# Xattn and FFN block on one core: the router with its gate stationary in four column groups, and another order behind the last attention unit

## What is computed

```python
x = x + attention(layernorm(x), ctx, ...)          # [8, 128, 512]
xf = layernorm(x).reshape(-1, 512)
routing = softmax(xf @ gate_w.T, axis=1)           # 8 experts
in_scale, out_scale = routing @ in_channel_scale, routing @ out_channel_scale
out = (xf * in_scale) @ sign(weight).T * out_scale + bias
x = x + out
```

## Time and profile before

| | |
|---|---|
| median of 3 runs | 800.29 us |
| the profiled execution, its own time | 800.21 us |
| its span in the trace | 798.4 us |
| TensorE matmuls busy | 793.6 us, 99% |
| TensorE weight loads | 675.5 us, 85% |
| VectorE | 633.1 us, 79% |
| ScalarE | 352.9 us, 44% |
| GpSimd | 298.5 us, 37% |
| granted TensorE clock | 1.00 |

### The profile page before, as it was taken

How to read it: one execution, slowest core, us unless ns; L and a number is a source line. 1 busy time by engine, 2 the same in 40 slices (tenths; PEclk the granted TensorE clock), 3 DMA queues, 4 the chain that set the end, 5 groups by cost and what they waited for, 6 DMA issues and landing times.

```text
span 798.4 us, 12698 instructions
## 1 busy us (share of the span) xinstructions
PE 793.6 (99%) x4090; PEld 675.5 (85%) x4090; DVE 633.1 (79%) x1066; ACT 352.9 (44%) x949; POOL 298.5 (37%) x279
## 2 busy tenths in 40 slices
PE   9999999999999999999999999999999999999998
PEld 7888888888888888888888888888888888888886
DVE  6877878886893596889988879788877978877775
ACT  6633432432341253554534345343534434446683
POOL 3123021020111032746455446554544654434136
PEclk9999999999999999999999999999999999999999
DMA  8464674575456648627566666656665675653002
GB/s 302 146 200 171 223 247 137 177 256 171 154 183 212 210 160 274 212 68 233 168 216 206 195 183 200 224 153 212 199 213 154 207 225 159 200 195 139 1 1 106
DMA packets 103217, 145.54 MB, mean 182 GB/s; under 512 B 9944, under 2 KB 74584, under 8 KB 97648
## 3 DMA queue, kind: packets, MB, share of 16 engines
q1 hardware_dynamic: 102720, 144.33, 55.7%
q10 hardware_dynamic: 432, 0.39, 0.2%
HBM read 93.31 MB, written 51.38 MB: 181 GB/s over the span
## 4 chain that ended last, share of the span: by engine, by line
PE 98%; DMA 1%; DVE 0%; issue 0%; ACT 0%; SPq 0%; DVEq 0%
PE out L1470 11%; PE out L1472 11%; PE out L1471 11%; PE proj L1470 11%; PE proj L1472 11%; PE proj L1471 10%; PE s L1564 7%; PE o L1591 4%; PE s L1471 4%; PE s L1472 4%; PE s L1470 4%; PE t L1591 3%; PE proj L1667 1%; PE proj L1668 1%; PE t L1619 1%; PE t L1575 1%
## 5 line engine op out<-in xcount | busy, mean ns | idle before, releaser
L872 POOL TENSOR_TENSOR w_stage<-w_stage 128x256 f32<-128x256 f32 x30 | 26.9, 898 | 262.9 <-DMA w_stage<-in_wk 241.4
L896 POOL TENSOR_TENSOR bias_mask<-bias_raw,mask_neg 128x512 f32<-128x512 f32 x64 | 75.3, 1184 | 81.4 <-DVE s L1306 67.4
L1042 ACT ACTIVATE s<-s,neg_max 128x128 f32<-128x128 f32 x208 | 71.5, 349 | 52.5 <-DVE neg_max L1309 52.5
L1470 PE MATMUL out<-wo_hi,o_hi 128*128 128x512 f32 x224 | 88.5, 395 | 0.0
L1472 PE MATMUL out<-wo_lo,o_hi 128*128 128x512 f32 x224 | 87.8, 392 | 0.0
L1471 PE MATMUL out<-wo_hi,o_lo 128*128 128x512 f32 x224 | 87.3, 390 | 0.0
L1470 PE MATMUL proj<-x_hi,w_hi 128*128 128x512 f32 x210 | 85.0, 405 | 0.0
L884 POOL TENSOR_TENSOR w_lo<-w_stage,w_hi 128x512 fp32r<-128x512 f32 (+1 forms) x52 | 59.4, 1155 | 68.1 <-ACT w_hi L988 68.1
L1472 PE MATMUL proj<-x_lo,w_hi 128*128 128x512 f32 x210 | 82.5, 393 | 0.0
L1471 PE MATMUL proj<-x_hi,w_lo 128*128 128x512 f32 x210 | 82.0, 390 | 0.0
L1347 DVE TENSOR_TENSOR acc<-out,acc 128x512 f32<-128x512 f32 x100 | 67.2, 673 | 14.1 <-PE out L1472 14.0
(11 more groups left out here) (370 smaller groups left out, 2123.5 us busy)
## 6 DMA issues: line engine op xcount, KB each, us to landing
k_spill<-ring SPq DMA_DIRECT2D x64, 256.0 KB, 3.4
v_spill<-ring SPq DMA_DIRECT2D x64, 256.0 KB, 2.5
p_turned<-probs SPq DMA_DIRECT2D x208, 64.0 KB, 2.8
probs_t<-p_turned SPq DMA_DIRECT2D x52, 256.0 KB, 2.9
big_stage<-in_wv SPq DMA_DIRECT2D x8, 1024.0 KB, 8.7
w_stage<-in_wq SPq DMA_DIRECT2D x32, 256.0 KB, 3.5
k_first<-k_spill SPq DMA_DIRECT2D x8, 1024.0 KB, 7.3
v_first<-v_spill SPq DMA_DIRECT2D x8, 1024.0 KB, 9.7
```

The lines of the kernel that those rows point to most:

```text
L896: pool.tensor_tensor(bias_mask[:, j % 2], bias_raw[:, i % 2][:, None, :].to_broadcast([P, HALF, P]), mask_neg[:, halves[half], :], ALU.add ...
L1042: last = act.activation(scores_of(j)[:, b], scores_of(j)[:, b], ACT.Exp, bias=neg_max[:, col:col + 1], accum_out=row_sum[:, col:col + 1])
L1470: pe.matmul(to[:], left_hi, right_hi, start=first and n == 0, stop=False, skip_group_check=True)
```

## The change

The router's logits come about in another way. The gate becomes the stationary operand, padded with zeros to 32 columns (`COLS`), and the tile's transposed chunk is the moving one, 128 columns. A pair has two tiles of four chunks, so eight matmuls; they go to four groups of 32 columns of the array, and so to four groups of 32 partitions of `t_bank`, two chunks summed in each (G). VectorE copies that bank's 128 columns to SBUF (GC), and one matmul with a constant matrix of zeros and ones adds the chunks and turns the result to token by expert (GF); its 16 columns are what GM and GE read. The constant matrix is made once, by GATHER. `GA` is gone. `gate_sb` is cleared by GpSimd ahead of `scales_raw`, and the small loads wait for both.

The diff, cut to its core:

```diff
+COLS = 32
...
-    steps += [("SCALES",)]
+    steps += [("SCALES",), ("GATHER",)]
...
-        gate_sb, exps = sb("gate_sb", [P, DC, E], F32), sb("exps", [P, B, E], F32)
+        gate_sb, exps = sb("gate_sb", [P, DC, COLS], F32), sb("exps", [P, B, E], F32)
+        gather = sb("gather", [P, 2, E], F32)
...
+        part_logits = [probs[:, r, 0] for r in range(2)]
...
-        BY_DVE = (6,)
+        BY_DVE = (3, 2, 6, 7)
...
             def small_loads():
-                sp.wait_ge(g_clear, 1)
+                sp.wait_ge(g_clear, 2)
...
-                sp.dma_start(gate_sb[:], gate_t).then_inc(d_ffn_small, 16)
+                sp.dma_start(gate_sb[:, :, 0:E], gate_t).then_inc(d_ffn_small, 16)
...
+                pool.memset(gate_sb[:], 0.0).then_inc(g_clear, 1)
                 pool.memset(scales_raw[:], 0.0).then_inc(g_clear, 1)
...
-                dve.wait_ge(pe_nt, nth_tx["TX", i - HALF])
+                if i < HALF:
+                    dve.wait_ge(pe_s, last_score(LAST - 2))
+                else:
+                    dve.wait_ge(pe_nt, nth_tx["TX", i - HALF])
...
+            def gather_matrix():
+
+                dve.wait_ge(pe_prod, max(last_of(n) for n in range(PLAIN, NKV)))
+                units = ident[:].rearrange("p (r k e) -> p r e k", r=2, k=2)[:, :, 0:E]
+                dve.tensor_reduce(gather[:], units, axis=AX.X, op=ALU.add).then_inc(v_gather, 1)
+
+            def partial_logits(p):
+                dve.wait_ge(pe_part, p + 1)
+                if p == 0:
+                    dve.wait_ge(pe_t, nth_t["T", len(UNITS) - 1])
+                if p >= 2:
+                    dve.wait_ge(pe_gate, p - 1)
+                dve.tensor_scalar(part_logits[p % 2], t_bank[:, 2 * P:3 * P], 1.0, None, ALU.mult).then_inc(v_part, 1)
...
+            def router(p):
+
+                if p == 0:
                     pe.wait_ge(d_ffn_small, 80)
...
+                to = t_bank if p else take(t_bank)
+                if p:
+                    pe.wait_ge(v_part, p)
+                for r in range(2):
+                    pe.wait_ge(a_nt, nth_txc["TXC", 2 * p + r])
+                for s in range(2):
+                    for group in range(4):
+                        r, c = group // 2, group % 2 * 2 + s
+                        rows = slice(group * COLS, (group + 1) * COLS)
+                        last = pe.matmul(to[rows, 2 * P:3 * P], gate_sb[:, c, :], nt_pairs[p][:, r, c * P:(c + 1) * P],
+                                         start=s == 0, stop=s == 1, tile_position=(0, group * COLS), skip_group_check=True)
+                last.then_inc(pe_part, 1)
+
+            def gather_logits(p):
+                if p == 0:
+                    pe.wait_ge(v_gather, 1)
+                pe.wait_ge(v_part, p + 1)
+                if p:
+                    take(t_bank)
+                pe.matmul(t_bank[:, 0:2 * E], part_logits[p % 2], gather[:].rearrange("p r e -> p (r e)"), start=True,
+                          stop=True).then_inc(pe_gate, 1)
+                read_by(t_bank, a_rexp, p + 1)
```

More of the change, by code:

```diff
@@ L339, in schedule @@
     steps = [part for step in steps for part in parts_of(step)]
-    steps += [("PV", 60), ("S", 62), ("N", 61), ("OH", 60), ("S", 63), ("SC", 62), ("T", 61), ("OUT", 15, 1), ("OL", 60), ("EXP", 62),
-              ("BM", 63), ("SC", 63), ("OUT", 15, 0), ("PT", 61), ("ADD", 15, 1), ("EXP", 63), ("OUT", 15, 2), ("ADD", 15, 0), ("N", 62),
[17 rows of a table removed]
-              ("SUM", 5), ("OS", 7), ("MP", 6), ("M", 7, 1), ("OSC", 7), ("SUM", 6), ("M", 7, 0), ("MPL", 1), ("SUML", 1), ("MPL", 0),
-              ("SUML", 0)]
+    steps += [("PV", 60), ("S", 62), ("N", 61), ("OH", 60), ("S", 63), ("SC", 62), ("T", 61), ("OUT", 15, 1), ("OL", 60), ("EXP", 62), ("BM", 63),
[18 rows of a table added]
+              ("MPL", 0), ("SUML", 0), ("MPL", 1), ("SUML", 1), ("MP", 6), ("SUM", 6)]
     return steps
@@ L457, in xattn_ffn @@
         probs, bias_raw = sb("probs", [P, 2, HALF, P], F32), sb("bias_raw", [P, 2, P], F32)
-        gap = sb("gap", [P, 12 * 256 - 3 * D - B * STACK - DC * E - B * E - 2 * P], F32)
+        gap = sb("gap", [P, 12 * 256 - 3 * D - B * STACK - DC * COLS - B * E - 2 * P - 2 * E], F32)
         probs_t = sb("probs_t", [P, 2, HALF * P], F32)
@@ L523, in xattn_ffn @@
         v_last_res, v_n, v_ones = sem("v_last_res"), sem("v_n"), sem("v_ones")
+        v_gather, pe_part, v_part = sem("v_gather"), sem("pe_part"), sem("v_part")
         v_vsum, v_vs4, v_xsum, v_res = sem("v_vsum"), sem("v_vs4"), sem("v_xsum"), sem("v_res")
@@ L1381, in route @@
                 if p == 0:
-                    dve.wait_ge(g_clear, 2)
+                    dve.wait_ge(g_clear, 3)
                 link(dve.reciprocal(exps_inv[:, pair], exps_sum[:, pair]))
@@ L1447, in _ @@
                   "OL": out_low, "ADD": add_out, "ST": ffn_statistics, "LN2": ffn_norms, "LS": normal_scales, "NT": normal_tile,
-                  "GM": logit_maxima, "ROUTE": route, "Y": scale_tiles, "YL": scaled_low, "MP": scale_product, "SUM": last_sums,
+                  "GATHER": gather_matrix, "GC": partial_logits, "GM": logit_maxima, "ROUTE": route, "Y": scale_tiles, "YL": scaled_low, "MP": scale_product, "SUM": last_sums,
                   "MPL": last_scale_product, "SUML": last_sum})
@@ L1611, in ffn_transpose @@
                 read_by(ffn_bank(i), a_nt, nth_txc["TXC", i])
-            def router(p, r):
-                if p == 0 and r == 0:
+            def router(p):
+                if p == 0:
                     pe.wait_ge(d_ffn_small, 80)
[L1616 to L1629, removed]
+                to = t_bank if p else take(t_bank)
[19 more added lines that the diff above has]
+                read_by(t_bank, a_rexp, p + 1)
             def transpose_routing(p):
@@ L1683, in _ @@
             walk({"WARM": warm_up, "D": plain_product, "P": product, "S": score, "T": transpose_probs,
-                  "PV": probs_times_values, "OUT": output, "TX": ffn_transpose, "GA": first_router, "G": second_router, "RT": transpose_routing,
+                  "PV": probs_times_values, "OUT": output, "TX": ffn_transpose, "G": router, "GF": gather_logits, "RT": transpose_routing,
                   "R": routed_scales, "OS": routed_out_scale, "M": ffn_product})
```

## The result

The changed kernel takes 802.02 us, the median of 13 runs (801.47 to 802.67), against 800.29 (799.97 to 800.69) for the kernel before: a ratio of 1.0023, interval 1.0014 to 1.0031. It is slower, by 1.7 us. The forecast was 800.6, the range 797.7 to 802.5.

What follows compares the result with a forecast made beforehand. It took TensorE, busy 99% of the span, as the bound. Terms: -7.15 - 0.43 + 5.2 + 1.3 + 1.43 = +0.35 us on 800.21, giving 800.56, or 800.6 against the median; range 797.7 to 802.5.

Steps and rivals of the forecast that it cites:

- the signs that I had named for being wrong: In the changed kernel's chain: G near 0.45 us, TensorE ending before 792, or M-block waits for MP or YL.
- Removed: Old router matmuls on TensorE: 6.48 us of passes plus 0.67 of longer slots behind them, 7.15 us gone.
- G at 1.0: Eight two-pass router matmuls per pair on TensorE: 1.0 us, only neighbouring passes overlapping; bounds 0.45 and 1.78.
- GF at 0.30 a pair: The gathering matmul on TensorE: two passes, 0.20 us, and 0.10 on the next slot, per pair.
- side by side: Rival on the G blocks: four column groups run truly in parallel, G costs 0.45, total 798.4 us; chance 0.28.
- Emptying at a change: Rival: each of eight changes between whole array and parts exposes 0.165 us, +1.3, total 801.9; chance 0.12.
- Wait (a): TensorE before G of pair 0, which needs both copies TXC 0 and 1: 0.36 us later start.
- Wait (b): GF 0 and 1 on TensorE wait for VectorE's copy GC, taken as 0.25 us: 0.17 and 0.13, together 0.30.
- Wait (c): TX 7 on TensorE waits because VectorE's normalising of tiles takes 1.5 us each beside GpSimd's work: 0.65 us.
- Waits in the M blocks for routing, YL and MP: TensorE's product blocks: no wait for MP or YL, proj banks free by the queues before M takes them; zero.
- The end: From TensorE's last product slot to VectorE's end 2.62 us for 1.29, 1.33 more; with the larger store 1.43.
- Off the path: ScalarE and VectorE shifts, GATHER, the gate's clear and load, and reordered MP and SUM: all hidden, nothing added.

Runs made afterwards that it cites:

- e6: The changed kernel with the router matmuls of a pair issued group after group instead of round the four groups: 802.05 us, ratio 1.0018.
- e8: The changed kernel with buffers in their old places, the other order of last sums, and GpSimd's BI 0, BI 1 and BI 4 earlier: 797.72 us, ratio 0.9968.
- e3: The changed kernel with SUM 4 ahead of SUM 5, and MP 6 and SUM 6 ahead of tile 7's halves: 800.22 us, ratio 0.9997.
- e1: The kernel before, with only buffers moved: probs_t to routing and the gate 448 bytes per partition lower, exps 64 bytes lower: 801.99 us, ratio 1.0016.
- e2: The changed kernel with gate and gather matrix directly behind the gap, all other buffers in their old places, two waits added: 800.84 us, ratio 1.0004.
- after: The changed kernel itself, with the new router and order, against the kernel before: 802.02 us, ratio 1.0023.
- e5: The changed kernel with tiles 6 and 7 normalised on ScalarE again, tiles 2 and 3 staying on VectorE: 802.76 us, ratio 1.0031.

## Why the prediction was right, and where it was wrong

The range held, and the sign of my sum was right: +0.35 us by its terms, +2.3 between the profiles, +1.7 between the medians. That is in good part luck. The forecast was for no change that can be told, and the terms were off in both directions: the router was 1.2 us cheaper than I had it, and three other terms together 3.15 us dearer. Without the router's share the others would have carried the time to about 803.2, out of the range. Of the signs that I had named for being wrong, two are there: G is nearer to 0.45 than to 1.0, and the M blocks wait for YL and MP.

- **Removed, 7.15 us**: nothing in the runs speaks against it; with it the balance of TensorE from T 63 on closes to 0.04 us.
- **G at 1.0 and GF at 0.30 a pair, 5.2 us: wrong, 4.0 measured.** The step that failed is the reason I gave, that passes of one matmul follow each other and TensorE starts in order, so that only neighbours overlap. Measured: 0.57 for sixteen passes, and 0.59 with the group's passes in a row (experiment e6). The rival *side by side* had the mechanism (0.45 and 798.4); the time did not follow because the other terms ate it. The Trainium skill (TensorEngine Tiling, Key Properties) says that different tiles load and multiply in parallel; the trace agrees, sixteen passes in 0.57 us. The Trainium skill (TensorE: Matmul & The Clock Gate, Part 3) says that matmuls keep strict order. My 1.0 came from this order and from my own step that a second pass holds up all behind it until its first is done. The trace has starts 7 ns apart within a round, so nothing is held up in that way; whether the order is kept, its records do not tell.
- **Emptying at a change**: 0.09 before and 0.10 behind a G, so 0.8 us over four pairs. I gave it a chance of 0.12 as a rival with 1.3 us; something of the kind is there, and smaller. But the old blocks, on the whole array, had 0.67 us of longer slots behind them as well, and GF has them too; only the 0.09 ahead of a G is new. The rule of the Trainium skill (TensorEngine Tiling, Key Properties) that switching the tiling mode drains TensorE fits with these 0.09; no run here separates draining from another cause.
- **Wait (a), G 0: 0.36 predicted, 0.26 measured. Wait (b), GC: 0.25 predicted, 0.28 measured; 0.12 of wait at TX 3** stands for the 0.30 I had for GF.
- **Wait (c), TX 7: 0.65 predicted, 0.97 measured.** The mechanism was right in its place and price: NT 6 and NT 7 at 1.39 and 1.41 beside GpSimd, 0.53 and 0.54 without (experiment e8, which has the wait gone). The Trainium skill (SBUF — State Buffer, SBUF: two separate sides) describes a port pair that VectorE and GpSimd share as a lock held for the whole instruction; the trace agrees: both NT end 0.3 us after the GpSimd operation they stood beside, and neither is merely slowed.
- **Waits in the M blocks for routing, YL and MP: zero predicted, 1.22 measured** (0.52, 0.36, 0.34). This step failed in "by the queues each is free before M takes it": I followed the order, but priced the small operations at their undisturbed times, while ROUTE 3 took 1.48 and YL 3 1.07 beside GpSimd, and MP 5 stood 1.64 us behind a sum of GpSimd. A stall that I had used for NT holds for other operations on VectorE as well.
- **The end: 1.43 predicted, 1.71 measured.** Step right, size short by 0.3: one more sum, 0.93 instead of 0.42, ran beside GpSimd's last one. Experiment e3 takes 1.5 us of it away.
- **"Off the path": nothing predicted, 1.2 us measured, as much as any other miss.** I priced the gate's clear, load and DMA runs, but not that a buffer in front of others moves them. Neither a step nor a rival held it (experiments e1 and e2). Another 0.37 us from the first 7 us of the span is the execution's own: the same figure is +0.09 in experiment e3, whose instructions there are those of after. In after the chain has two slots of 0.61 and 0.43 us there (at 6.11 and 6.72) where their kind takes 0.23, so TensorE seems to have come to its full speed a little later; that was not tested.

The errors sum up: -1.16 for G and GF, +1.26 for waits, +0.28 for the end, +1.61 ahead of T 63: +1.99, on +0.35 makes 2.34, against 2.31. The chance of "slower" was 0.23. It was too low by what I had left at zero: moved buffers, and chains that only hid under the old blocks.

## What to carry to other kernels

When work is taken from the bounding engine, list what each removed block covered: here the shorter router alone lost 1.6 us, because its new copy held up VectorE's queue, the routing chain behind it had grown and its cover had shrunk. When VectorE's operations between buffers must be quick, put GpSimd's elementwise work elsewhere in time; moving three adds gained 1.6 us by the medians. And a changed buffer size is a change of every address behind it: compare the addresses as well as the code, and look at matmul distances for a drift that no wait shows.

## What the runs showed of the hardware that was not expected

- Two-pass fp32 matmuls on four column groups overlap about threefold, in both orders that were tried: 0.57 and 0.59 us for sixteen passes of 128 columns (0.76 with the longer slots around them), where sixteen whole-array passes at 0.111 would take 1.78.
- The slot ahead of a block on column groups is about 0.1 us longer. So is the one behind it, but that holds for the old block on the whole array as well.
- Even a small VectorE operation can take as long as the GpSimd operation beside it: 1.35 us for the first of ROUTE 3's two operations of 16 columns, beside an add of 1.30. Not every one does: the product of 512 columns out of PSUM at 782.11, beside GpSimd's YP 1, took its usual 0.68.
- After a wait of 1.94 us in experiment e5 TensorE's granted clock was 0.50 (1.2 GHz) for 3.4 us.
- A shift of operands by 448 bytes per partition made some TensorE matmuls 2 to 3 ns slower (227.3 to 230.1 in one group, 242.7 to 244.7 in another), one by 512 bytes did not (227.4). Its cause stays open.
